# Attention normalised on the probabilities instead of the output, values turned into the stationary operand, in a one-core tokenizer, attention and expert kernel

## The chip, the cores and the metric

The kernel runs on one core of a Trainium2 chip. The metric is the device time of one execution in microseconds (us). The engines are PE (TensorE, matrix multiply), DVE (VectorE), ACT (ScalarE), POOL (GpSimd) and SP (SyncE, which only issues transfers). Each engine works through its own queue in order, and the kernel orders engines against each other with semaphores written by hand.

## The reference, cut to what matters

An input of 64 sequences is cut into 93 overlapping patches each (a strided product), goes through a causal attention layer with 8 heads of 64 and a bias by distance, and then through a two-of-sixteen expert layer. The change is inside the attention:

```python
tokens = jnp.einsum('bnpd,edp->bne', patches, Wr) + b           # 64 x 93 x 128
q = _split_heads(_proj(xp, wq1, wqd), b, n) * scale             # 8 heads of 64
k = _split_heads(_proj(xp, wk1, wkd), b, n)
v = _split_heads(_proj(xp, wv1, wvd), b, n)
sim = jnp.einsum('bhid,bhjd->bhij', q, k)                       # 93 x 93 per head
sim = sim + bias[None, None] * slopes[None, :, None, None]
attn = jax.nn.softmax(sim, axis=-1)
out = jnp.einsum('bhij,bhjd->bhid', attn, v)
return out.transpose(0, 2, 1, 3).reshape(b, n, INNER) @ wout.T
```

## The kernel before, in words

The 64 sequences form 16 groups of four. Phase 1 is a software pipeline over tiles: `step(t, u, f)` runs, for tile number t, six stages on six different groups: token product (group t, `tok`), layer norm (t-1, `norm`), the query, key and value projections with their three-tap convolution (t-2, `proj`), attention (t-3, `attn`), gating (t-4, `gate`), and the scatter of the rows to their experts (t-5, `scat`). Each tile has four steps s = 0 to 3, and each step takes one sequence through attention; n counts them (64 in all). Every engine has its own `step` with the same loops, and what stands in that text is its queue: nothing reorders it. t runs from 0 to 20; at t = 5 to 15 all six stages are on. At t = 17 and 18 attention still runs, without token product and norm. Phase 2 (experts, output) comes after, and waits until all rows are scattered.

In one step before the change:

- PE turns the shifted scores of the sequence before (L452, eight 93x93 transposes into `psS`), turns the values of this one (L469), multiplies turned probabilities by values with the probabilities stationary (L500, 65 columns: 64 values and a column of ones that yields the sum of the exponentials), forms the scores with bias (L516, L521), turns the normalised output (L544) and multiplies it by `wout` (L576). Between them stand three projection products `proj` and four token products `tok_taps`, each three matmuls at L406, L407 and L408.
- DVE takes the row maxima `rmax` of the scores (L876), subtracts them (L879, `shifted`), later takes the reciprocal of the sums (L867) and multiplies the output by it (L870, `attn`), runs two of three convolution taps for three blocks (`conv`, L831 and L834 each), and adds the result to the residual (L891). Once per tile come the layer norm statistics (`stats`, twice, L841 and L845), `route`, `choose`, `rank` and `place` (L898 to L954).
- ACT forms the exponentials while it moves the turned scores out of `psS` (L700, `probT`), moves the values (L710) and the turned output (L746), runs the third tap (`tap2`, L675) and rounds the input (`high`, L667, `x_hi`). `normalise` applies the two layer norms.
- POOL forms the rest of the rounded input (`low`, L1043, `x_lo`) and of the normalised tokens (L1096, `xnT_lo`), the small chain of a layer norm (L1066 to L1085, starting with `veps`) and issues the scatters (L1106), two per step, or eight in a row at the head of the tile where `norm` is off (t from 17).

`psP` has two buffers, so a projection product waits for the convolution two blocks back: `wait(pe, conv_done, (t - 2) * NBLK + (k - 1))`. The scatter waits for `slot_done`, which `place` gives, and PE turns `rw` (L536) after `rw_done`, the last result of `place`. That `rwT` is what phase 2 weighs the experts with.

Of the kernel before, what the change touches and what calls it, by code (L numbers as in the profile page):

```python
# [33 lines left out]
NT = 93  # L34
# [23 lines left out]
def build(nc, x, w_tok, b_tok, gamma, beta, wq, wk, wv, cq, ck, cv, w_out, w_gate, w1, w2,  # L58
# [3 lines left out]
    with ctx:  # L62
# [41 lines left out]
        vrow = [sb(f"vrow{u}", [NT, H, DH + 1]) for u in range(2)]  # L104
        rmax = sb("rmax", [NT, 2, 4])
        shifted = sb("shifted", [NT, 2, 4, NT])
        probT = sb("probT", [NT, 2, 4, NT])
        rden = sb("rden", [NT, 2, 4])
        attn = sb("attn", [NT, H * DH])
# [50 lines left out]
        with ExitStack() as phase1:  # L160
# [24 lines left out]
        psTot = psO[:, 0, 264:264 + E]  # L185
# [20 lines left out]
        consts_ready, zeros_ready, taps_ready, bias_cast, vones_ready, rwzero_ready = (  # L206
            sem("consts_ready"), sem("zeros_ready"), sem("taps_ready"), sem("bias_cast"),
            sem("vones_ready"), sem("rwzero_ready"))
# [11 lines left out]
        p_tr, p_evac, pv_mm, den_done, norm_done = (  # L220
            sem("p_tr"), sem("p_evac"), sem("pv_mm"), sem("den_done"), sem("norm_done"))
        a_tr, a_evac, out_mm, res_add = sem("a_tr"), sem("a_evac"), sem("out_mm"), sem("res_add")
# [180 lines left out]
        def _(pe):  # L403
# [38 lines left out]

            def step(t, u, f):
                for s in range(GB):
                    n = (t - 3) * GB + s
                    prev = f.attn and s > 0 or f.last and s == 0
                    if prev:

                        pe.wait_ge(shift_done, n)
                        for a in range(2):  # L450
                            for hh in range(4):
                                mm = nc.tensor.transpose(psS[:NT, a, hh * NT:(hh + 1) * NT], shifted[:, a, hh, :],  # L452
                                                         ident[:NT, :NT])
                            mm.then_inc(p_tr, 1)
                    if f.gate and s == 2:
                        wait(pe, hn_ready, t - 3)
                        wait(pe, norm_done, n - 1 if f.attn else B)
                        for b in range(GB):
                            mm = nc.tensor.transpose(psHn[:, b * NT:(b + 1) * NT], hn[u][:, b, :],
                                                     ident[:NT, :NT])  # L460
                        mm.then_inc(hnT_tr, 1)
                    if f.proj and s == 0:
                        proj(t, u, f, 3 * s)
                    if f.attn:
                        if s == 0:
                            pe.wait_ge(conv_done, (t - 2) * NBLK)
                        wait(pe, a_evac, n - 1)
                        for j in range(QB):
                            mm = nc.tensor.transpose(psV[:NT, j * 128:(j + 1) * 128],  # L469
                                                     qkv[1 - u][:, 2 * QB + j, s, :], ident[:, :])  # L470
                        mm.then_inc(v_tr, 1)
                    if f.proj and s > 0:
                        proj(t, u, f, 3 * s)
# [10 lines left out]
                    if f.tok:  # L484
                        tok_taps(t, s, 0, 1)
                    if prev:

                        pe.wait_ge(p_evac, n * 2)
                        pe.wait_ge(v_evac, n)
                        wait(pe, norm_done, n - 1)  # L490

                        wait(pe, res_add, n - 1)
                        if f.gate and s == 2:
                            wait(pe, hnT_evac, t - 3)
                        if f.gate and s == 3:
                            wait(pe, logit_copy, t - 3)
                        if f.scat and s == 0:
                            wait(pe, pos_done, t - 4)
                        for h in range(H):
                            mm = nc.tensor.matmul(psO[:NT, h // 4, (h % 4) * (DH + 1):(h % 4 + 1) * (DH + 1)],  # L500
                                                  probT[:, h % 2, h // 2, :], vrow[(s + 1) % 2][:, h, :],
                                                  start=True, stop=True)
                        mm.then_inc(pv_mm, 1)
# [6 lines left out]
                    if f.attn:  # L510

                        if s == 0 and isinstance(t, int) and t == 3:
                            pe.wait_ge(bias_cast, 4)
                        wait(pe, p_evac, n * 2)
                        for a in range(2):
                            nc.tensor.matmul(psS[:NT, a, 0:4 * NT], ident16[:NT, :NT], bias[:, a, :],  # L516
                                             start=True, stop=False, skip_group_check=True)
                        for hh in range(4):
                            for a in range(2):
# [8 lines left out]
                    if f.tok:  # L528
                        tok_taps(t, s, 1, 2)
                    if f.attn and prev:  # L530
                        pe.wait_ge(v_evac, n + 1)
                    if f.scat and s == 0:
# [5 lines left out]
                        if not prev:  # L538
                            mm.then_inc(rwT_tr, 1)
# [120 lines left out]
        def _(ac):  # L660
# [31 lines left out]
            def step(t, u, f):  # L692
                for s in range(GB):
# [19 lines left out]
                    if f.proj:  # L713
                        tap2(t, u, 3 * s)
# [458 lines left out]
```

## Time and profile before

| | |
|---|---|
| median of 3 runs | 843.96 us (843.8 to 844.66) |
| the profiled execution, its own time | 846.1 us |
| span of its instructions | 844.4 us |
| mean granted TensorE clock | 0.943 |
| PE busy | 752.6 us (89% of the span) |
| DVE busy | 615.9 us (73%) |
| ACT busy | 468.9 us (56%) |
| POOL busy | 383.3 us (45%) |
| one full tile of four steps | 36.61 us |

Busy times are of the whole span; phase 1 ends near 694 us and phase 2 follows. A PE that shows as busy is not necessarily at its peak, and the shares are means over stretches that have different limits, so the stretches are read one by one below. In the rows of groups, "busy" is the time of all instructions of the group, then the mean of one in ns.

### The profile page before, as it was taken

Reading aid. Unit: us, or ns where it says so; the run is one execution under the profiler, and the core shown is the slowest. Engines: PE = TensorE matmul, PEld = TensorE weight load, DVE = VectorE, ACT = ScalarE, POOL = GpSimd, SP = SyncE. Lnnn points to the kernel's source line nnn. Section 1 sums busy time; section 2 is a strip of 40 time slices with the busy share of each in tenths; the row PEclk is TensorE's granted clock in tenths of the full one; section 3 lists DMA queues with packets and bytes.
Section 4 is the critical chain, followed back from the end, with each engine's and each line's share of the span. In section 5 each row is a group of like instructions: output and inputs, shape, how many; then the busy total and the mean of one; then the engine's idle time right before and its main releaser. Section 6 shows DMA issues by size and latency. Waiting matters only on the chain. (4 is left out here: it accounts for less than half of the span.)

```text
span 844.4 us, 20971 instructions
## 1 busy us (share of the span) xinstructions
PE 752.6 (89%) x6670; PEld 696.4 (82%) x6670; DVE 615.9 (73%) x1621; ACT 468.9 (56%) x1021; POOL 383.3 (45%) x408
## 2 busy tenths in 40 slices
PE   5577999999999999999999999999786318999987
PEld 5466999999999999999999999977675208999983
DVE  2145778888888888888888888899573145888865
ACT  3345566656566665656666566555333107899950
POOL 3442243666556565555656556545241552222200
PEclk9787999999999999999999999999898658999989
DMA  6321123332112112111212211050000022222205
GB/s 190 99 72 46 47 72 117 102 104 64 48 47 66 47 47 65 50 46 46 68 46 50 65 48 48 19 208 20 10 15 6 19 69 73 64 62 62 62 17 145
DMA packets 42246, 53.89 MB, mean 64 GB/s; under 512 B 13651, under 2 KB 28947, under 8 KB 41680
## 3 DMA queue, kind: packets, MB, share of 16 engines
q1 hardware_dynamic: 26304, 37.13, 15.5%
q0 software_dynamic: 13120, 14.05, 6.0%
q10 hardware_dynamic: 2768, 2.00, 0.8%
q8 instruction: 32, 0.52, 0.3%
q14 instruction: 22, 0.18, 0.1%
HBM read 42.69 MB, written 10.26 MB: 63 GB/s over the span
## 5 line engine op out<-in xcount | busy, mean ns | idle before, releaser
L1106 POOL DMA_INDIRECT expert_rows<-hn,slot x128 | 167.7, 1310 | 92.5 <-DVE slot L951 59.9
L1043 POOL TENSOR_TENSOR x_lo<-x_raw,x_hi 128x752 fp32r<-128x752 f32 x64 | 114.9, 1795 | 151.7 <-ACT x_hi L667 151.7
L831 DVE SCALAR_TENSOR_TENSOR qkv<-ps,taps,qkv 128x368 f32<-128x368 f32 x192 | 114.0, 594 | 86.2 <-ACT qkv L675 84.6
L675 ACT ACTIVATE qkv<-ps,taps 128x372 f32<-128x372 f32 x192 | 108.6, 567 | 90.1 <-PE ps L408 89.8
L834 DVE SCALAR_TENSOR_TENSOR qkv<-ps,taps,qkv 128x364 f32<-128x364 f32 x192 | 114.6, 597 | 6.8
L406 PE MATMUL ps<-x_hi,wtok_hi 128*128 128x376 f32 x256 | 95.3, 372 | 11.3 <-DVE wtok_lo L811 9.0
L500 PEld LDWEIGHTS psO<-vrow,probT 93*93 93x93 f32 x1024 | 93.5, 162 | 4.7 <-ACT probT L700 3.2
L500 PE MATMUL psO<-vrow,probT 93*93 93x65 f32 x1024 | 93.9, 245 | 2.0 <-ACT probT L700 1.1
L407 PE MATMUL ps<-x_lo,wtok_hi 128*128 128x376 f32 x256 | 89.1, 348 | 0.0
L408 PE MATMUL ps<-x_hi,wtok_lo 128*128 128x376 f32 x256 | 89.0, 348 | 0.0
L576 PE MATMUL psO<-wout,attnT 128*93 128x128 f32 x512 | 70.6, 283 | 18.6 <-ACT attnT L746 15.8
L998 DVE TENSOR_REDUCE qkv<-qkv 128x512 f32 (+1 forms) x108 | 72.3, 681 | 19.1 <-ACT qkv L771 18.6
L406 PE MATMUL ps<-xnT_hi,wqkv_hi 128*128 128x372 f32 x192 | 78.0, 406 | 9.0 <-DVE qkv L834 5.0
L576 PEld LDWEIGHTS psO<-wout,attnT 128*93 128x93 f32 x512 | 63.8, 167 | 22.4 <-ACT attnT L746 19.8
L700 ACT ACTIVATE probT<-psS 93x372 f32<-93x372 f32 x128 | 54.4, 472 | 47.9 <-PE psS L452 47.6
L312 POOL DMA_DIRECT2D xs<-expert_rows x54 | 29.8, 552 | 82.2 <-PE psS L595 41.3
L407 PE MATMUL ps<-xnT_lo,wqkv_hi 128*128 128x372 f32 x192 | 65.0, 339 | 0.0
L408 PE MATMUL ps<-xnT_hi,wqkv_lo 128*128 128x372 f32 x192 | 65.0, 338 | 0.0
L876 DVE TENSOR_REDUCE rmax<-psS 93x8 f32<-93x744 f32 x64 | 59.2, 926 | 7.0 <-PE psS L521 5.9
L667 ACT ACTIVATE x_hi<-x_raw 128x752 fp32r<-128x752 f32 x64 | 52.7, 823 | 19.1 <-DMA x_raw<-in_x 14.4
L879 DVE TENSOR_TENSOR shifted<-psS,rmax 93x744 f32<-93x744 f32 x64 | 59.4, 929 | 5.2
L521 PEld LDWEIGHTS psS<-qkv 64*93 64x93 f32 x1024 | 47.2, 158 | 18.2 <-issue 18.2
(160 smaller groups left out, 1620.7 us busy)
## 6 DMA issues: line engine op xcount, KB each, us to landing
x_raw<-in_x SPq DMA_DIRECT2D x64, 376.0 KB, 3.2
w1s<-in_w POOLq DMA_DIRECT2D x8, 512.0 KB, 4.9
w<-in_w SPq DMA_DIRECT2D x4, 1024.0 KB, 10.3
xs<-expert_rows SPq DMA_DIRECT2D x54, 64.0 KB, 1.8
xs<-expert_rows POOLq DMA_DIRECT2D x54, 64.0 KB, 2.1
out<-resid SPq DMA_DIRECT2D x16, 160.0 KB, 2.4
expert_rows<-hn,slot POOLq DMA_INDIRECT x128, 3.5
qkv<-in_w_tok ACTq DMA_DIRECT2D x4, 256.0 KB, 6.7
```

The source lines that it names most:

```text
L406: nc.tensor.matmul(dst, w_hi, x_hi, start=start, stop=False)
L407: nc.tensor.matmul(dst, w_hi, x_lo, start=False, stop=False)
L408: return nc.tensor.matmul(dst, w_lo, x_hi, start=False, stop=stop)
L500: mm = nc.tensor.matmul(psO[:NT, h // 4, (h % 4) * (DH + 1):(h % 4 + 1) * (DH + 1)], probT[:, h % 2, h // 2, :], vrow[(s + 1) % 2][:, h, : ...
L576: mm = nc.tensor.matmul(psWout, attnT[:, j, :], wout[:, j, :], start=(j == 0), stop=(j == QB - 1))
L675: nc.scalar.activation(qkv[u][:, k, :, :], psP[(k + 1) % 2][:, 0:GT].rearrange("p (b n) -> p b n", n=NT), ACT.Copy, scale=taps[:, k, 2:3]) ...
L831: nc.vector.scalar_tensor_tensor(dst[:, :, 1:NT], src[:, :, 0:NT - 1], taps[:, k, 1:2], dst[:, :, 1:NT], ALU.mult, ALU.add).then_inc(tap1_ ...
L834: nc.vector.scalar_tensor_tensor(dst[:, :, 2:NT], src[:, :, 0:NT - 2], taps[:, k, 0:1], dst[:, :, 2:NT], ALU.mult, ALU.add).then_inc(conv_ ...
L879: nc.vector.tensor_tensor(shifted[:, :, :, :], heads(psS, NT), rmax[:, :, :].unsqueeze(3).broadcast_to([NT, 2, 4, NT]), ALU.subtract).then ...
L998: nc.vector.tensor_reduce(part[:, bass.ds(i, 1), :].rearrange("p i j -> p (i j)"), act[k][:, :].rearrange("p (j n) -> p j n", n=128), AXX, ...
L1043: nc.gpsimd.tensor_tensor(x_lo[u][:, 0:PIECE], x_raw[u][:, :], x_hi[u][:, 0:PIECE].bitcast(F32), ALU.subtract)\
L1106: nc.gpsimd.indirect_dma_start(rows, bass.IndirectOffsetOnAxis(slot[1 - u][:, c:c + 1], 0), hn[1 - u][:, c % GB, :], None)\
```

## The change

The exponentials are now formed before the turn, with queries on partitions, and divided by their row sums there. The pieces:

- ACT forms the exponentials in place in `prob` (93x744, two buffers), one instruction per step, and its move out of `psS` becomes a plain copy.
- DVE sums `prob` per head (`den`), takes the reciprocal and multiplies the four heads of the odd half (`a = 1`) in place; POOL multiplies the even half. The reciprocal and the product on the output, and the column of ones, are gone.
- PE turns the normalised probabilities and multiplies with the values stationary (64 columns wide, two halves of the array in turn), which gives the output already turned, in bank 0 of `psO`. The four transposes L544 are gone; ACT moves `psO` to `attnT`.
- The order of every queue in `step` is rewritten. DVE's `place` moves from the head of step 0 behind the product on the odd heads; ACT's `high` moves to the head, its `normalise` to the end of a step; on POOL the product on the even heads stands between `x_lo` and the scatters.

```diff
+            def turn_prob(f, s, n):
+                if f.attn:
+                    pe.wait_ge(shift_done, n + 1)
+                for a in range(2):
+                    pe.wait_ge((even_ready, odd_ready)[a], n)
+                    for hh in range(4):
+                        mm = nc.tensor.transpose(psS[:NT, a, hh * NT:(hh + 1) * NT], prob[(s + 1) % 2][:, a, hh, :],
+                                                 ident[:NT, :NT])
+                    mm.then_inc(p_tr, 1)
+            def weigh(s, n):
+                pe.wait_ge(p_evac, n * 2)
+                pe.wait_ge(v_evac, n)
+                wait(pe, a_evac, n - 1)
+                wait(pe, res_add, n - 1)
+                for hh in range(4):
+                    for a in range(2):
+                        mm = nc.tensor.matmul(psO[64 * a:64 * a + 64, 0, hh * NT:(hh + 1) * NT],
+                                              vrow[(s + 1) % 2][:, 2 * hh + a, :], probT[:, a, hh, :],
+                                              start=True, stop=True)
+                mm.then_inc(pv_mm, 1)
...
                     if f.scat and s == 0:
                         wait(pe, rw_done, t - 4)
-                        wait(pe, a_evac, n - 1 if prev else B)
...
                     if prev:
-                        pe.wait_ge(norm_done, n)
-                        for j in range(QB):
-                            mm = nc.tensor.transpose(psV[:, j * NT:(j + 1) * NT], attn[:, j * 128:(j + 1) * 128],
-                                                     ident[:NT, :NT])
-                        mm.then_inc(a_tr, 1)
+                        weigh(s, n)
...
+                    if f.attn:
+                        ac.wait_ge(shift_done, n + 1)
+                        p = prob[s % 2][:, :, :, :].rearrange("p a h n -> p (a h n)")
+                        nc.scalar.activation(p, p, ACT.Exp).then_inc(exp_done, 1)
...
-                        nc.vector.tensor_tensor(attn[:, :].rearrange("p (a h d) -> p a h d", a=2, d=DH),
-                                                o[:, :, :, 0:DH],
-                                                rden[:, :, :].unsqueeze(3).broadcast_to([NT, 2, 4, DH]),
-                                                ALU.mult).then_inc(norm_done, 1)
...
+                    if f.attn:
+                        dve.wait_ge(exp_done, n + 1)
+                        wait(dve, even_ready, n)
+                        nc.vector.tensor_reduce(den[:, :, :], prob[s % 2][:, :, :, :], AXX, ALU.add).then_inc(sum_done, 1)
+                        dve.wait_ge(sum_done, n + 1)
+                        nc.vector.reciprocal(rden[:, :, :], den[:, :, :]).then_inc(rden_done, 1)
+                        dve.wait_ge(rden_done, n + 1)
+                        p = prob[s % 2][:, 1, :, :]
+                        nc.vector.tensor_tensor(p, p, rden[:, 1, :].unsqueeze(2).broadcast_to([NT, 4, NT]), ALU.mult)\
+                            .then_inc(odd_ready, 1)
+                    if f.scat and s == 0:
+                        place(t - 5, 1 - u)
...
+                    if f.attn:
+                        pool.wait_ge(rden_done, n + 1)
+                        p = prob[s % 2][:, 0, :, :]
+                        nc.gpsimd.tensor_tensor(p, p, rden[:, 0, :].unsqueeze(2).broadcast_to([NT, 4, NT]), ALU.mult)\
+                            .then_inc(even_ready, 1)
                     if f.scat and f.norm:
                         scatter(t - 5, u, 2 * s, 2)
```

DVE's queue in step 0 of a full tile (t = 5), before, from the end of the tile before; `wden` to `rw` is `place`, the two rows with `qkv` are one `conv`:

```order
L891 TENSOR_TENSOR resid<-psO,resid 93x128
L934 TENSOR_SCALAR wden<-egap 93x4
L936 RECIPROCAL wts<-wden 93x4
...
L954 TENSOR_TENSOR rw<-wsel 93x4x16
L831 SCALAR_TENSOR_TENSOR qkv<-ps,taps,qkv 128x4x92
L834 SCALAR_TENSOR_TENSOR qkv<-ps,taps,qkv 128x4x91
L867 RECIPROCAL rden<-psO 93x8
L870 TENSOR_TENSOR attn<-psO,rden 93x512
L876 TENSOR_REDUCE rmax<-psS 93x8
L879 TENSOR_TENSOR shifted<-psS,rmax 93x744
```

And the same engine in the same step of the changed kernel:

```order
L848 TENSOR_REDUCE rmax<-psS 93x8
L851 TENSOR_TENSOR prob<-psS,rmax 93x744
L825 SCALAR_TENSOR_TENSOR qkv<-ps,taps,qkv 128x4x92
L828 SCALAR_TENSOR_TENSOR qkv<-ps,taps,qkv 128x4x91
L867 TENSOR_REDUCE den<-prob 93x8
L869 RECIPROCAL rden<-den 93x8
L872 TENSOR_TENSOR prob<-prob,rden 93x372
L928 TENSOR_SCALAR wden<-egap 93x4
...
L945 CAST slot<-slotf 93x8
L948 TENSOR_TENSOR rw<-wsel 93x4x16
L825 SCALAR_TENSOR_TENSOR qkv<-ps,taps,qkv 128x4x92
```

The maxima moved to the head of the step, one `conv` now stands between the subtraction and the new sum, and `place` moved from the head of the step to behind seven other instructions (a `...` in the first fence leaves out `place`'s middle rows).

PE's queue of the changed kernel in the same step, from the turn of the probabilities; L543 is the turn of `rw`, L493 is `weigh`, and three rows with `ps` are one product:

```order
L481 MATMUL psS<-ident,prob 93x93 x8
L406 MATMUL ps<-xnT_hi,wqkv_hi 128x372
L407 MATMUL ps<-xnT_lo,wqkv_hi 128x372
L408 MATMUL ps<-xnT_hi,wqkv_lo 128x372
L406 MATMUL ps<-x_hi,wtok_hi 128x376
L407 MATMUL ps<-x_lo,wtok_hi 128x376
L408 MATMUL ps<-x_hi,wtok_lo 128x376
L543 MATMUL psV<-ident,rw 128x93
L493 MATMUL psO<-probT,vrow 64x93 x8
```

The turn of `rw` stands in front of `weigh`, and so in front of everything that PE does in the rest of that step; before, it stood behind the product of probabilities and values.

POOL's queue of the changed kernel at the head of tile 17 and up to tile 18, where `norm` is off (L1096 is here the product on the even heads):

```order
L1106 DMA expert_rows<-hn,slot 97408x128 x10
L1096 TENSOR_TENSOR prob<-prob,rden 93x372
L1072 TENSOR_SCALAR veps<-mv 93x4
L1074 TENSOR_SCALAR nmean<-mv 93x4
L1077 TENSOR_TENSOR rstd<-veps,half 93x4
L1080 TENSOR_TENSOR shift<-nmean,rstd 93x4
L1096 TENSOR_TENSOR prob<-prob,rden 93x372 x3
```

Eight of the ten scatters in the first row belong to tile 17; the product of step 0 has moved in behind them, where before only the layer norm chain stood.

## Rows read from the trace of the kernel before

**Rows 1.** Windows: us, then busy time of each engine, clock, DMA
```profile
293.60:330.21 36.61, 36.61 (x347) 34.59 (x346) 30.99 (x88) 22.37 (x47) 21.70 (x22) 1.00 0.20 53
553.36:585.77 32.41, 29.82 (x297) 25.62 (x295) 30.29 (x88) 18.01 (x41) 14.61 (x18) 1.00 0.26 91
585.77:625.34 39.57, 31.97 (x284) 28.36 (x284) 28.20 (x78) 15.56 (x34) 12.22 (x13) 0.87 0.05 11
625.34:652.59 27.25, 18.94 (x188) 16.70 (x189) 12.27 (x41) 7.79 (x18) 9.55 (x11) 0.87 0.06 15
```

**Rows 2.** Timeline, weight loads of PE in one step: start, us
```profile
339.79 1.49 PEld L500 LDWEIGHTS psO<-vrow,probT 93*93 93x93 f32 x16
341.20 0.18 PEld L516 LDWEIGHTS psS<-bias,ident 93*93 93x93 bf16 x2
341.66 0.74 PEld L521 LDWEIGHTS psS<-qkv 64*93 64x93 f32 x16 [0.28 <-issue]
342.49 0.19 PEld L406 LDWEIGHTS ps<-xnT_hi,wqkv_hi 128*128 128x128 f32 x1
...
343.99 0.47 PEld L544 LDWEIGHTS psV<-ident,attn 93*128 93x128 f32 x4
...
345.37 0.98 PEld L576 LDWEIGHTS psO<-wout,attnT 128*93 128x93 f32 x8
346.30 0.77 PEld L452 LDWEIGHTS psS<-ident,shifted 93*93 93x93 f32 x8
```

**Rows 3.** Timeline, DVE in steps 2, 3, 0 and 1
```profile
320.60 0.21 DVE L898 COPY logit<-psO 93x64 f32<-93x64 f32 x1
...
322.88 0.59 DVE L831 SCALAR_TENSOR_TENSOR qkv<-ps,taps,qkv 128x368 f32<-128x368 f32 x1
...
324.02 0.19 DVE L867 RECIPROCAL rden<-psO 93x8 f32<-93x8 f32 x1
...
324.86 0.92 DVE L876 TENSOR_REDUCE rmax<-psS 93x8 f32<-93x744 f32 x1
325.90 0.93 DVE L879 TENSOR_TENSOR shifted<-psS,rmax 93x744 f32<-93x744 f32 x1
326.75 0.21 DVE L925 TENSOR_TENSOR pos<-psO,base 93x64 f32<-93x64 f32 x1
...
329.60 0.28 DVE L891 TENSOR_TENSOR resid<-psO,resid 93x128 f32 x1
329.80 0.21 DVE L934 TENSOR_SCALAR wden<-egap 93x4 f32<-93x4 f32 x1
...
331.03 0.22 DVE L954 TENSOR_TENSOR rw<-wsel 93x64 f32<-93x64 f32 x1
...
339.32 0.87 DVE L841 BATCH_NORM_STATS2 stat<-resid 93x6 f32 x4
...
340.64 0.57 DVE L831 SCALAR_TENSOR_TENSOR qkv<-ps,taps,qkv 128x368 f32<-128x368 f32 x1
```

**Rows 4.** Instructions of one line: min/median/max ns, first and last start
```profile
L811 DVE TENSOR_TENSOR wtok_lo<-qkv,wtok_hi x4: 678/686/1918, 7.0 to 10.3; 128x512 fp32r<-128x512 f32 x4
```

**Rows 5.** Groups of the profile page, ACT
```profile
L675 ACT ACTIVATE qkv<-ps,taps 128x372 f32<-128x372 f32 x192 | 108.6, 567 | 90.1 <-PE ps L408 89.8
L667 ACT ACTIVATE x_hi<-x_raw 128x752 fp32r<-128x752 f32 x64 | 52.7, 823 | 19.1 <-DMA x_raw<-in_x 14.4
```

**Rows 6.** Timeline, POOL
```profile
6.60 1.76 POOL L1043 TENSOR_TENSOR x_lo<-x_raw,x_hi 128x752 fp32r<-128x752 f32 x1 [5.59 <-ACT x_hi L667]
...
327.04 1.00 POOL L1096 TENSOR_TENSOR xnT_lo<-xnT,xnT_hi 128x372 fp32r<-128x372 f32 x1
...
340.92 0.19 POOL L1077 TENSOR_SCALAR veps<-mv 93x4 f32<-93x4 f32 x1 [3.20 <-DVE mv L845]
...
342.61 1.81 POOL L1043 TENSOR_TENSOR x_lo<-x_raw,x_hi 128x752 fp32r<-128x752 f32 x1
...
583.42 1.29 POOL L1106 DMA_INDIRECT expert_rows<-hn,slot  x1 [2.40 <-DVE slot L951]
```

More of the change, by code:

```diff
@@ new lines, in values @@
+            def values(t, u, f, s, n):
+                if s == 0:
+                    pe.wait_ge(conv_done, (t - 2) * NBLK)
+                wait(pe, v_evac, n)
+                if f.scat and s == 1:
+                    wait(pe, rwT_evac, t - 4)
+                for j in range(QB):
+                    mm = nc.tensor.transpose(psV[:NT, j * 128:(j + 1) * 128],
+                                             qkv[1 - u][:, 2 * QB + j, s, :], ident[:, :])
+                mm.then_inc(v_tr, 1)
+            def turn_prob(f, s, n):
+                if f.attn:
+                    pe.wait_ge(shift_done, n + 1)
+                for a in range(2):
+                    pe.wait_ge((even_ready, odd_ready)[a], n)
[3 more added lines that the diff above has]
+                    mm.then_inc(p_tr, 1)
@@ L446, in step @@
                     prev = f.attn and s > 0 or f.last and s == 0
[L447 to L452, printed above, removed]
-                                                         ident[:NT, :NT])
[L454 to L462, printed above, removed]
+                    if f.attn:
+                        scores(t, u, s, n)
+                    if f.proj:
                         proj(t, u, f, 3 * s)
                     if f.attn:
-                        if s == 0:
-                            pe.wait_ge(conv_done, (t - 2) * NBLK)
-                        wait(pe, a_evac, n - 1)
-                        for j in range(QB):
[L469 to L473, printed above, removed]
+                        values(t, u, f, s, n)
                     if f.norm and s == 0:
@@ L483, in step @@
                         mm.then_inc(tok_tr, 1)
[L484 to L503, printed above, removed]
                     if f.norm and s == 3:
@@ L572, in step @@
                         pe.wait_ge(a_evac, n)
-                        if f.gate and s == 3:
-                            wait(pe, base_done, t - 3)
                         for j in range(QB):
@@ L752, in step @@
                         tap2(t, u, 3 * s + 2)
+                    if f.norm and s == 2:
+                        normalise(t - 1, rstd, shift, xn, ln_shift, xn_ready)
+                    if f.gate and s == 1:
+                        wait(ac, scattered[u], (t - u - 4) * (16 * GB))
+                        normalise(t - 4, rstd2, shift2, hn[u], ln2_shift, hn_ready)
                     if isinstance(t, int) and t == 0 and s == GB - 1:
@@ L1059, in step @@
                 for s in range(GB):
+                    n = (t - 3) * GB + s
                     if f.scat and not f.norm and s == 0:
```

160 lines of the change are left out of this document (74 added, 86 removed).

## The prediction, made before the changed kernel was run

> **What bounds it now.** I read the windows first, cut at the same point of two successive tiles. In a full tile (36.61 us) PE is busy for all of it and DVE for 30.99 us; with the token product over, a tile takes 32.41 us with DVE busy 30.29 and PE 29.82 [rows 1]. So the eleven full tiles (t = 5 to 15) and the two before them are bound by PE, with DVE close behind, and tile 16 by DVE. Next the timelines, for what one block costs in its queue, counted from its start to the start of the next. PE: the score block 1.29 us (341.20 to 342.49), three products 1.50 (0.50 each), probabilities times values 1.41, `wout` 0.93, the four transposes of the output at most 0.47, the eight of the scores some 0.7 [rows 2]. DVE: maxima 1.04, subtraction 0.85, one `conv` 1.14, reciprocal with product on the output 0.84, residual 0.20; and once per tile `place` 1.45, `stats` twice 1.32, `route` with `choose` 2.28, `rank` 0.21 [rows 3]. Check: 4 x (1.04 + 0.85 + 3 x 1.14 + 0.84 + 0.20) + 6.58 = 32.0 us, which is the 32.41 us of the tile that DVE bounds.
>
> **The change, part by part.**
>
> PE loses 0.45 us per step with the transposes. `weigh` has no row of its kind. The nearest are the scores: eight pairs in two halves of the array take 0.83 us, with 0.28 us of idle time ahead of them as the array changes its form, so 1.1; if the halves don't overlap it stays at the old 1.41. I take 1.1. PE alone would give 36.6 - 4 x 0.75 = 33.6 us per tile.
>
> DVE loses 0.84 and gets: the sum over 744 elements, priced as the maxima over as many, 1.04; the reciprocal, 0.19 and a small gap, 0.23; the product on the odd heads. The last from two rows: 512 elements took 0.686 us [rows 4], 744 took 0.93, so 1.05 ns per element and 0.54 for 372, of which the next instruction covers 0.08 as it does behind the subtraction: 0.46. A step is then 7.24 instead of 6.35 us, and a tile 4 x 7.24 + 6.58 = 35.5 us. DVE, not PE, bounds the tile from here, and its best case is 1.1 us under today's 36.6.
>
> ACT gets 0.82 us per step (its 752-column copy took 0.823 [rows 5]), 22.37 + 3.3 of some 40 us: not a bound, but the sum on DVE waits for it.
>
> POOL gets the even heads, 1.00 us per step by the 372-column `x_lo` kind [rows 6], 21.70 + 4 of 40 us: hidden in itself.
>
> **Waits that are new.** I lay out each step from the start of the maxima (0). The subtraction ends at 1.9. PE turns the previous probabilities (2.6), does two products (3.6), `weigh` (4.7), two products (5.7), `wout` (6.6) and the next scores (7.9; with the tail of a matmul 8.1). Where DVE has more than that to do, DVE sets the step.
>
> Step 0: PE's turn of `rw` stands ahead of `weigh` and waits for the end of `place`, which now stands behind the odd heads. ACT has `tap2` (0.57), the values and the residual copy (512 columns each, some 0.6 between the rows of 372 and 752 columns [rows 5]) ahead of the exponentials. The first product of the step is through at 0.7, so these end at 2.5 and the exponentials at 3.3; sum 4.35, reciprocal 4.6, odd heads 5.05, `place` 6.5. PE then needs `rw` 0.15, `weigh` 1.1, two products 1.0, `wout` 0.93, scores 1.3: 11.1 us in all. Queued behind that wait are the product whose `conv` DVE wants next, and the scores. Before, `place` ran at the head of step 0, straight behind the residual (329.60, 329.80 [rows 3]).
>
> Step 1: 7.24 + 1.32 = 8.6 us. Step 2: 8.6 + 1.6 (`route`) = 10.2. Step 3: DVE 7.24 + 0.67 + 0.21 = 8.1, PE 8.1 and the ranking's matmuls 0.3: 8.4. Together 38.3 us, 1.7 more than now.
>
> Then the collisions. One of four equal DVE subtractions with both inputs in SBUF took 1918 ns where the others took 686 [rows 4]. It started at 7.0, while POOL was in `x_lo` from 6.60 to 8.36 [rows 6]: it ended 0.56 us after POOL, as if it had begun there. The product on the odd heads is such an instruction. In steps 1 and 2 POOL starts its layer norm chain 0.3 us after DVE has gone on from `stats` (340.92 [rows 6], 340.64 [rows 3]), and `x_lo` follows 1.7 us later for 1.8 us (342.61 [rows 6]). From the maxima: DVE goes on at 1.9 + 1.32 = 3.2, the chain starts at 3.5, `x_lo` runs from 5.2 to 7.0; the odd heads would start at 3.2 + 1.14 + 1.04 + 0.23 = 5.6 and end at 7.4 instead of 6.2. That is 1.2 us in each of the two steps, and DVE is the bound in both. In step 0 POOL's even heads (5.1 to 6.1) hold up `place`, 0.6; in step 3 `x_lo` and `xnT_lo` hold up `choose`, 0.3. In all 3.3 us: 38.3 + 3.3 = 41.6.
>
> The Trainium skill states the same in SBUF — State Buffer, section "SBUF: two separate sides": the pair of ports that VectorE and GpSimd share is taken for a whole instruction, and a VectorE instruction needs it with two SBUF inputs. The trace agrees, 1918 against 686 ns. By that rule the sum, with one SBUF input, is free of it; and if the even heads took the pair first when `x_lo` ends, the odd ones would lose a further 1.0 us.
>
> **The sum.** Full tiles: 11 x (41.6 - 36.6) = 55. Tile 4 (no scatter, so no wait for `rw`): step 0 8.3, then 9.8, 11.4, 8.7, 38.2: +2. Tile 3 +1. Tile 16, without token product: 10.7 + 8.6 + 10.2 + 8.4 against 32.4: +5. Tiles 17 and 18: eight scatters now stand ahead of the even heads of step 0, and wait for `slot`, from 6.3. Eight take 8 x 1.6 = 12.7 us (a scatter 1.29 [rows 6] and 0.3 to the next), then the heads 1.0: ready at 20. PE needs 6.3 from there through turn, copy, `weigh`, `wout` and scores. So steps 0 and 1 take 26 us; with steps 2 and 3 (8.9 and 8.2) tile 17 is 43.4 against 39.57, tile 18 with 26 and 8.5 is 34.5 to its third step against 27.25 [rows 1]. That is +11, and `place` for tile 19 starts 3 later: +14, of which I take 12 since these tiles have other slack. Phase 2 unchanged. 55 + 2 + 1 + 5 + 12 = 75. The profiled execution took 846.1 us (span 844.4), 2 above the median of the runs: 921 there, 919 as a median.
>
> **Rivals.**
> - *The collisions hardly bite* (`x_lo` lies elsewhere, or the delay is shared): tiles of 38.3, 11 x 1.7 = 19, tiles 3 and 4 nothing, 5 and 12 as before: +36, 880. For it: `x_lo` is placed by several waits, and only one clear case is in the trace. Against: the window of 1.8 us is wide. Chance 0.24, with all that lies between 865 and 895.
> - *TensorE's clock falls too.* In tile 17, with PE busy 31.97 of 39.57 us, the mean granted clock was 0.87; tile 16, at 29.82 of 32.41, kept 1.00 [rows 1]. The changed tile would have PE busy near 34 of 41.6. A quarter of the tiles' PE path at a lower clock adds 1 to 3 us each: 935 to 955. Chance 0.11.
> - *Faster.* DVE packs without a wait: 35.5 us per tile, 13 x 1.1 = -14 us, with the last tiles at +5: 835. It decides where the new waits of a tile stay under 1.1 us together; the wait for `rw` alone costs 2. For it: PE really has less to do, and ACT and POOL have room. Chance 0.06, up to 842.
> - *Nothing to measure* (within 0.2%, which is what a measurement of this kernel can tell from no change): the same with 1 us of waits per tile; 0.03.
>
> **Numbers.** The layout with collisions has 0.56, its own range 895 to 940. With the rival without collisions inside, 868 to 945 leaves about 2 in 10 out. Slower 0.91, same 0.03, faster 0.06.
>
> **What would show it.** Windows of a full tile near 41.6 us, DVE busy over 85% and PE under 90%. PE idle ahead of the turn of `rw`, released by DVE's `rw`, 3 us per full tile. The odd product with a median near 0.55 us and a maximum near 1.8, long in steps 1 and 2. `den` near 0.93 us, eight pairs of `weigh` near 0.83. PE idle ahead of the turn of `prob` in tiles 17 and 18, released by POOL, some 8 us each. Wrong would make it: `weigh` at twice its price matters little; an `x_lo` that comes before the odd product costs 2.4 us of my tile; an exponential that waits behind other work on ACT would add to every step.

## The result, and the profile after

The changed kernel takes 970.5 us (median of 4 runs, 963.67 to 977.35) against 843.88 us of the kernel before: 1.150 times as long, 95% interval 1.141 to 1.160. The sign was forecast; the size was not: 970.5 lies above the range of 868 to 945 and 51 us above the 919 expected. The four runs lie 13.7 us apart, and the interval of their ratio is 8 us wide to either side, so a difference from 970.5 below is sure to some 8 us only; where a trace shows the same saving, its number stands beside it. The profiled execution took 966.65 us, its span is 964.9 us.

The head of its page: busy time, share of the span, instructions; then the granted clock in 40 slices.

```profile
span 964.9 us, 20730 instructions
...
PE 771.0 (80%) x6414; PEld 676.5 (70%) x6414; DVE 715.3 (74%) x1683; ACT 518.3 (54%) x1085; POOL 453.4 (47%) x472
...
PEclk9899989898979998999998899899787555999999
```

No engine is busy as large a share of the time as PE was before (89%): the kernel now waits. The windows, cut at PE's turn of `rw` in successive tiles, answer to [rows 1] (us, busy time and instructions of PE, PEld, DVE, ACT, POOL, clock, DMA share, GB/s):

```profile
285.32:330.95 45.63, 37.98 (x329) 33.34 (x329) 38.29 (x92) 25.51 (x51) 26.15 (x25) 0.92 0.16 43
330.95:377.41 46.46, 36.86 (x329) 32.03 (x329) 38.34 (x92) 25.43 (x51) 26.15 (x25) 0.93 0.16 42
```

A full tile takes 46 us where it took 36.61 and was forecast at 41.6. DVE is busy for 38.3 of them; forecast were 35.5 plus the time in collisions. The clock, 1.00 before, is 0.92. Where the time went along the program is read from an instruction that closes each tile in both kernels, the last addition to the residual. Timeline of the changed kernel at the ends of tiles 4, 15, 16 and 18, then of the kernel before:

```profile
139.36 0.28 DVE L885 TENSOR_TENSOR resid<-psO,resid 93x128 f32<-93x128 f32 x1
...
642.28 0.28 DVE L885 TENSOR_TENSOR resid<-psO,resid 93x128 f32<-93x128 f32 x1
...
682.51 0.28 DVE L885 TENSOR_TENSOR resid<-psO,resid 93x128 f32<-93x128 f32 x1
...
776.84 0.29 DVE L885 TENSOR_TENSOR resid<-psO,resid 93x128 f32<-93x128 f32 x1 [1.77 <-PE psO L574]
```

```profile
146.47 0.28 DVE L891 TENSOR_TENSOR resid<-psO,resid 93x128 f32<-93x128 f32 x1
...
549.37 0.28 DVE L891 TENSOR_TENSOR resid<-psO,resid 93x128 f32<-93x128 f32 x1
...
581.78 0.28 DVE L891 TENSOR_TENSOR resid<-psO,resid 93x128 f32<-93x128 f32 x1
...
655.96 0.29 DVE L891 TENSOR_TENSOR resid<-psO,resid 93x128 f32<-93x128 f32 x1 [1.27 <-PE psO L576]
```

Between the first two of each lie the eleven full tiles: 502.9 us after (45.7 each), 402.9 before (36.6 each), so +100.0. The next tile took 40.2 against 32.4 us, +7.8; the two behind it 94.3 against 74.2, +20.2. At the end of tile 4 the changed kernel is 7.1 us ahead. Together +120.9 us, and by that the second part of the kernel starts later (818.50 against 697.69); its own length has not changed.

One full tile on DVE, cut to the rows that matter. Step 1 starts at 291.30, step 2 at 301.06, step 3 at 314.03, the next tile's step 0 at 323.91 and its step 1 at 335.42:

```profile
291.30 0.93 DVE L848 TENSOR_REDUCE rmax<-psS 93x8 f32<-93x744 f32 x1
...
295.62 0.92 DVE L867 TENSOR_REDUCE den<-prob 93x8 f32<-93x744 f32 x1
...
296.80 1.86 DVE L872 TENSOR_TENSOR prob<-prob,rden 93x372 f32<-93x372 f32 x1
...
301.06 0.92 DVE L848 TENSOR_REDUCE rmax<-psS 93x8 f32<-93x744 f32 x1
...
312.33 1.77 DVE L901 TENSOR_TENSOR gap<-top 93x4 f32<-93x4 f32 x1
314.03 0.92 DVE L848 TENSOR_REDUCE rmax<-psS 93x8 f32<-93x744 f32 x1
...
323.91 0.93 DVE L848 TENSOR_REDUCE rmax<-psS 93x8 f32<-93x744 f32 x1
...
328.51 0.54 DVE L872 TENSOR_TENSOR prob<-prob,rden 93x372 f32<-93x372 f32 x1
328.97 0.77 DVE L928 TENSOR_SCALAR wden<-egap 93x4 f32<-93x4 f32 x1
```

And POOL in the same tile:

```profile
296.48 1.78 POOL L1037 TENSOR_TENSOR x_lo<-x_raw,x_hi 128x752 fp32r<-128x752 f32 x1
298.23 1.10 POOL L1096 TENSOR_TENSOR prob<-prob,rden 93x372 f32<-93x372 f32 x1
...
312.28 1.79 POOL L1037 TENSOR_TENSOR x_lo<-x_raw,x_hi 128x752 fp32r<-128x752 f32 x1
...
328.56 1.16 POOL L1096 TENSOR_TENSOR prob<-prob,rden 93x372 f32<-93x372 f32 x1 [3.06 <-DVE rden L869]
```

Three DVE instructions last about as long as POOL needs to the end of its own: the odd product (1.86 us, alone 0.54), as forecast; `wden` (0.77, alone 0.15), as forecast for `place` though a different line of it; and `gap`, 93 x 4 elements, 1.77 us instead of 0.14, in a place for which the prediction had no collision. It began 0.05 us behind an `x_lo`.

PE in the same stretch, behind the wait for `rw` and behind the turn in step 3:

```profile
285.32 0.41 PE L543 MATMUL psV<-ident,rw 93*128 93x93 f32 x1 [2.53 <-DVE rw L948]
...
287.59 0.52 PE L407 MATMUL ps<-x_lo,wtok_hi 128*128 128x376 f32 x1
287.90 0.52 PE L408 MATMUL ps<-x_hi,wtok_lo 128*128 128x376 f32 x1
288.21 0.51 PE L406 MATMUL ps<-xnT_hi,wqkv_hi 128*128 128x372 f32 x1
...
316.06 1.41 PE L481 MATMUL psS<-ident,prob 93*93 93x93 f32 x8 [3.45 <-DVE prob L851]
...
317.64 0.51 PE L407 MATMUL ps<-xnT_lo,wqkv_hi 128*128 128x372 f32 x1
317.95 0.51 PE L408 MATMUL ps<-xnT_hi,wqkv_lo 128*128 128x372 f32 x1
318.25 0.52 PE L406 MATMUL ps<-x_hi,wtok_hi 128*128 128x376 f32 x1
```

In both stretches the products follow one another at 0.31 us; elsewhere in this trace it is 0.17 (273.29, 273.46, 273.63). That is the lower of the clock's two levels, 1.2 instead of 2.4 GHz. Not every wait is followed by it: behind the same wait in the next tile, 2.68 us at 330.95, the products stand 0.17 apart. And in the tile shown the lower level had begun before the wait, at 282.28, behind a wait of 2.00 us for `prob` at 280.61. The waits of PE in all, by what ended them (us, times, longest):

```profile
PE psS L481 <- DVE prob L851: 69.2, 39, 4.0
PE psV L543 <- DVE rw L948: 38.8, 16, 3.2
...
PE psS L481 <- POOL prob L1096: 12.0, 2, 6.2
```

### The profile page after: what moved, and what is told of

Same layout as the page of the kernel before. It is cut to its first block and busy times, and to the rows that moved or that the text cites. A ratio compares the mean times of both kernels' runs of the same rounds, so it can differ in the third digit from the quotient of the medians.

```text
span 964.9 us, 20730 instructions
## 1 busy us (share of the span) xinstructions
PE 771.0 (80%) x6414; PEld 676.5 (70%) x6414; DVE 715.3 (74%) x1683; ACT 518.3 (54%) x1085; POOL 453.4 (47%) x472
## 5 line engine op out<-in xcount | busy, mean ns | idle before, releaser
L1096 POOL TENSOR_TENSOR prob<-prob,rden 93x372 f32<-93x372 f32 x64 | 70.3, 1099 | 140.5 <-DVE rden L869 140.4
L481 PE MATMUL psS<-ident,prob 93*93 93x93 f32 x512 | 63.6, 274 | 81.2 <-DVE prob L851 69.2
L481 PEld LDWEIGHTS psS<-ident,prob 93*93 93x93 f32 x512 | 53.5, 179 | 96.6 <-DVE prob L851 83.4
L406 PE MATMUL ps<-x_hi,wtok_hi 128*128 128x376 f32 x256 | 101.5, 396 | 11.0 <-DVE wtok_lo L805 8.8
L719 ACT ACTIVATE prob<-prob 93x744 f32<-93x744 f32 x64 | 52.7, 823 | 66.9 <-DVE prob L851 66.4
L574 PE MATMUL psO<-wout,attnT 128*93 128x128 f32 x512 | 80.0, 308 | 1.8 <-ACT attnT L737 1.7
L574 PEld LDWEIGHTS psO<-wout,attnT 128*93 128x93 f32 x512 | 75.1, 189 | 3.8 <-ACT attnT L737 2.8
L493 PE MATMUL psO<-probT,vrow 93*64 93x93 f32 x1024 | 69.9, 291 | 1.3 <-ACT probT L724 1.1
L493 PEld LDWEIGHTS psO<-probT,vrow 93*64 93x64 f32 x1024 | 56.4, 168 | 17.8 <-issue 12.8
L872 DVE TENSOR_TENSOR prob<-prob,rden 93x372 f32<-93x372 f32 x64 | 67.0, 1046 | 2.2
```

The source lines that it names most:

```text
L406: nc.tensor.matmul(dst, w_hi, x_hi, start=start, stop=False)
L493: mm = nc.tensor.matmul(psO[64 * a:64 * a + 64, 0, hh * NT:(hh + 1) * NT], vrow[(s + 1) % 2][:, 2 * hh + a, :], probT[:, a, hh, :], start= ...
L574: mm = nc.tensor.matmul(psWout, attnT[:, j, :], wout[:, j, :], start=(j == 0), stop=(j == QB - 1))
```

## The experiments

Four kernels first, to price what the prediction had named: the collision of the odd product, the wait for `rw`, the scatters. All times are medians; ratios are to the kernel before, beside which each ran (844.0 to 844.5 us).

**x_lo first.** On POOL, `low` stands ahead of the layer norm chain instead of behind it.

```
                     if f.scat and not f.norm and s == 0:
                         scatter(t - 5, u, 0, 2 * GB)
+                    if f.tok and f.more(t, s):
+                        low(t * GB + (s + 1), (s + 1) % 2)
...
-                    if f.tok and f.more(t, s):
-                        low(t * GB + (s + 1), (s + 1) % 2)
```

> Only the order of POOL's queue changes: in every step x_lo is formed ahead of the layer norm chain, so that in steps 1 and 2 it is over before DVE's product on the odd heads begins. Theory of the collisions: the 26 long odd products (1.75 to 1.89 us) become 0.54, worth 26 x 1.25 = 33 us, of which DVE as the bound of those steps gives back nearly all: 25 to 33 us faster than the changed kernel (970.5), the full tiles near 43 us. Rival, that the long products only cover other waits: the odd products are short but the time moves by less than 8 us. The collision of the gap instruction in step 2 (1.76 us) and that of wden in step 0 (0.77) stay under both.

Measured: 936.06 us, ratio 1.107 (1.103 to 1.111), 34.4 us less. The line of the odd product, min/median/max, in the changed kernel and here:

```profile
L872 DVE TENSOR_TENSOR prob<-prob,rden x64: 541/542/1887, 71.5 to 772.6; 93x372 f32<-93x372 f32 x64
```

```profile
L872 DVE TENSOR_TENSOR prob<-prob,rden x64: 541/542/544, 71.9 to 745.6; 93x372 f32<-93x372 f32 x64
```

No long one is left. In the changed kernel the 64 of them were busy for 67.0 us, 32.3 more than 64 x 0.542: nearly all that the time fell by. `gap` still collides (median 1266 ns).

**rw late.** PE's turn of `rw`, and ACT's copy of it, move to the end of step 0, behind the scores.

```
-                    if f.scat and s == 0:
-                        wait(pe, rw_done, t - 4)
...
                         mm.then_inc(out_mm, 1)
+                    if f.scat and s == 0:
+                        wait(pe, rw_done, t - 4)
...
```

> PE's turn of rw moves behind the wout product at the end of step 0, and ACT's move of rwT behind its last tap2. Theory of the rw wait: PE no longer idles 3.0 us per full tile ahead of weigh in step 0, and step 0 (now 12.7 us, against 11.7 laid out) falls to about 9.3; 11 to 14 tiles x 3.0 to 3.4 = 33 to 45 us faster than 970.5. As the idle time goes, TensorE should stay at full clock in that stretch. Rival, that DVE bounds step 0 anyway, with the wait only in its shadow: under 12 us.

Measured: 936.48 us, ratio 1.110 (1.107 to 1.113), 34.0 us less, 2.1 in each of 16 tiles. The prediction had said that this wait costs 2 us a tile. The 2.1 are what is left of more: by the traces, step 0 of the eleven full tiles takes 35.9 us less in all, and step 3 takes 14.8 us more, where PE now waits some 3.5 us for `prob` and then runs at the lower level (217.96 to 227).

**Scatters behind.** In the two last tiles POOL takes the even heads before the eight scatters.

```
-                    if f.scat and not f.norm and s == 0:
-                        scatter(t - 5, u, 0, 2 * GB)
...
                             .then_inc(even_ready, 1)
+                    if f.scat and not f.norm and s == 0:
+                        scatter(t - 5, u, 0, 2 * GB)
```

> In tiles 17 and 18 the eight scatters of step 0 go behind the product on the even heads instead of ahead of it. Theory: PE no longer waits for POOL's even heads there (12.0 us in two waits), 10 to 14 us faster than 970.5. Rival, that the scatters end later and hold back the layer norm chain of step 1 by as much: under 3 us.

Measured: 959.61 us, ratio 1.136 (1.132 to 1.140), 10.9 us less; the prediction had 12. The traces show it where it was expected: from the maxima of step 0, tile 17 takes 40.9 instead of 46.7 us, and tile 18 34.3 instead of 38.7 to its last step. POOL and PE in the changed kernel, the last of eight scatters, the even heads, and PE behind them:

```profile
700.39 1.28 POOL L1106 DMA_INDIRECT expert_rows<-hn,slot  x1 [0.30 <-issue]
701.70 0.82 POOL L1096 TENSOR_TENSOR prob<-prob,rden 93x372 f32<-93x372 f32 x1
```

```profile
702.66 1.53 PE L481 MATMUL psS<-ident,prob 93*93 93x93 f32 x8 [5.81 <-POOL prob L1096]
```

**All three.**

> The three moves together. If the three causes are apart they add: 68 to 90 us off 970.5, 880 to 902. If PE's wait for rw and the collisions cover each other, less: 915 or more. What DVE has to do itself (35.5 us per tile by the sum of its blocks, plus the collisions of gap and wden) leaves it slower than before the change, 844.

Measured: 879.23 us, ratio 1.041 (1.038 to 1.044), 91.3 us less, where the three singly give 79.3. Each came out near its price in the prediction, 2.4 x 13 + 2 x 16 + 12 = 75 us, which is as much as its whole sum. Yet 35 us remain. So there are costs that it did not name. Two candidates were in the trace: `gap`, and the clock.

**gap late, alone.** `gap` moves from the end of `route` in step 2 to behind the mask in `choose`, in step 3; nothing else.

```
-                nc.vector.tensor_tensor(gap[:, :], top[:, :, 1], top[:, :, 0], ALU.subtract).then_inc(gap_done, 1)
...
                                         hot[:, GB:, :], ALU.add).then_inc(mask_done, 1)
+                nc.vector.tensor_tensor(gap[:, :], top[:, :, 1], top[:, :, 0], ALU.subtract).then_inc(gap_done, 1)
```

> The changed kernel as it is, with gap alone moved from the end of route to behind the mask in choose. It prices the one collision that the prediction's list did not have: gap at 1760 ns where it was 141. Theory (the wait is on the path of step 2, whose probabilities TensorE waits for): 1.6 us less in 16 tiles, 26 us, and the clock a little up: 935 to 950. Rival (gap's wait is hidden, or the following max waits instead for something else): within 6 us of 970.5.

Measured: 939.05 us, ratio 1.113 (1.110 to 1.116), 31.5 us less. In its trace:

```profile
L913 DVE TENSOR_TENSOR gap<-top x16: 152/155/1003, 130.4 to 771.9; 93x4 f32<-93x4 f32 x16
```

Step 2 now takes 11.27 us (334.81 to 346.08) instead of 12.96. Over the eleven full tiles step 2 takes 18.8 us less and step 3, where PE had waited behind `gap`, 6.8 less. Moving one instruction of 93 x 4 elements is worth as much as the collision of all odd products. On the kernel with all three mends, the same move:

> The three mends together, and the operation gap moved from the end of route to behind the mask in choose, in step 3, away from GpSimd's x_lo. Theory (the 1.27 us that gap took in place of 0.14 is on the path): 1.1 us less in about 17 tiles: 8 to 19 us less than 879.2, so 860 to 871. Rival (the wait is only moved to whatever VectorE's next operation with two inputs is, or step 3 has no room): within 4 us of 879.2.

Measured: 857.71 us, ratio 1.017 (1.014 to 1.021), 21.5 us less. The expectation's upper end was 19.

**PE kept busy.** The changed kernel, with matmuls that depend on nothing ahead of the two waits.

```
+            def idle_work(count):
+                for _ in range(count):
+                    nc.tensor.matmul(psTok[:, 384:512], ident16[:, :], ident16[:, :], start=True, stop=True,
+                                     skip_group_check=True)
...
+                        idle_work(16)
                         turn_prob(f, s, n)
...
+                        idle_work(40)
                         wait(pe, rw_done, t - 4)
```

> The changed kernel with idle matmuls on TensorE (ident16 against itself into a stretch of psTok that nothing reads): 16 ahead of every turn of the probabilities and 40 ahead of the wait for rw. They depend on nothing, so they run while TensorE waits for VectorE (3.78 us ahead of a turn in step 3, 3.02 us ahead of the turn of rw); the results are unused. Theory (the idle stretches halve TensorE's clock for the products behind them): granted clock back to 0.98 or more in a full tile, the odd and even heads' weight loads back to 0.17 us from about 0.31, some 1.0 to 1.2 us less in each of steps 0 and 3, so 20 to 35 us less than the 970.5 us: 936 to 950. Rival 1 (VectorE's collisions set the length, the low clock is in their shadow): clock up, time within 6 us of 970.5. Rival 2: the idle matmuls, where VectorE is in time, stand in TensorE's way: 16 of them take some 0.9 us in 68 steps, the time rises by 20 us or more.

They write into the bank in which the token product sums, and change the numbers that come out of it, against what the expectation says of that stretch. The instructions of the rest are the same. Measured: 951.8 us (942.0 to 956.1), ratio 1.129 (1.124 to 1.133), 18.7 us less, just under the 20 expected, with 1664 matmuls more. PE in step 3 of a tile:

```profile
312.67 0.90 PE L486 MATMUL psS<-ident,prob 93*93 93x93 f32 x8 [2.55 <-DVE prob L857]
...
313.60 0.33 PE L407 MATMUL ps<-xnT_lo,wqkv_hi 128*128 128x372 f32 x1
313.77 0.33 PE L408 MATMUL ps<-xnT_hi,wqkv_lo 128*128 128x372 f32 x1
```

The turn takes 0.90 instead of 1.41 us, products stand 0.17 apart, and step 3 takes 8.45 us (310.64 to 319.09) instead of 9.88. `gap` is as long as it was (median 1765 ns), so this gain is the clock's, less what the idle matmuls themselves cost. Over the eleven full tiles steps 3 take 6.6 us less and steps 0 6.3; the tiles from 16 gain as well (17: 44.1 instead of 46.7 us). The trace is that of the fastest of the four runs.

On the mended kernel the same device does harm:

> The three mends, gap late, and 16 idle matmuls ahead of each turn of the probabilities. Theory (in the mended kernel too the halved clock behind the wait for VectorE's subtraction costs the step): granted clock near 1.00, 10 to 25 us less than the same kernel without the idle matmuls: 840 to 860. Rival 1 (VectorE sets the step): clock up, time within 4 us. Rival 2 (the idle matmuls delay the turn): 10 us or more longer.

Measured: 870.58 us, ratio 1.030 (1.027 to 1.033), 12.9 us more than without. The clock rises from 0.92 to 0.941, but the waits there are shorter and the idle matmuls stand ahead of work that was ready: rival 2.

**Without the row sum.** What DVE's new sum costs, on the kernel with three mends and on that with `gap` late too. `den` is one column plus 1.0, so the true sums are left out.

```
-   nc.vector.tensor_reduce(den[:, :, :], prob[s % 2][:, :, :, :], AXX, ALU.add).then_inc(sum_done, 1)
+   nc.vector.tensor_scalar(den[:, :, :], prob[s % 2][:, :, :, 0], 1.0, None, ALU.add).then_inc(sum_done, 1)
```

> The three mends together (x_lo first, rw turned late, scatters behind the even product) with the sum over the 93 columns left out: VectorE writes one column of the probabilities plus 1.0 to den, an operation on 93 x 8 in place of the reduction of 93 x 744 at 0.914 us, so the probabilities are divided by a wrong number and the rest is done as before. Theory (VectorE's own work is what lengthens a step once the collisions are gone): about 0.75 us less in each of 68 steps, some 45 to 50 us less than 879.2: 829 to 840, at or under the kernel before. Rival (the wait for GpSimd's half or TensorE sets the step): less than 20 us of that shows, 860 or more.

Measured: 862.63 us, ratio 1.022 (1.019 to 1.024), 16.6 us less instead of 45 to 50. The theory fell: of the 48 us that DVE was spared (58.5 to 10.7 busy) a third showed.

> The three mends and gap late (857.7 us), with the sum over the 93 columns left out as in the run on the three mends alone (one column plus 1.0 in its place, so the probabilities are divided by a wrong number). Theory (with gap out of the way VectorE is still what a step waits for, 33 us of work in a tile of 36 to 37): 25 us or more less, 833 or under. Rival (TensorE, with its rounded products through ScalarE's tap, is now as long as VectorE; in the run without the sum VectorE waited 64.0 us in all for ScalarE's tap where it had waited 33.9 here): less than 15 us, 843 or more.

Measured: 834.73 us, ratio 0.989 (0.986 to 0.992), 23.0 us less: nearer to the theory's 25 than to the rival's 15, within neither. DVE's wait for ACT's tap says where the rest went; the kernel with `gap` late, and the same without the sum:

```profile
L825 DVE SCALAR_TENSOR_TENSOR qkv<-ps,taps,qkv 128x368 f32<-128x368 f32 x192 | 113.0, 588 | 33.9 <-ACT qkv L673 33.9
```

```profile
L825 DVE SCALAR_TENSOR_TENSOR qkv<-ps,taps,qkv 128x368 f32<-128x368 f32 x192 | 113.3, 590 | 59.8 <-ACT qkv L673 59.4
```

DVE is spared 48 us and waits 26 more for a tap that hangs on PE's products: the two engines are nearly level, and taking work off one shows by half. This version alone is faster than the kernel before, by 1.1%, and only because it leaves the sum out.

**All on DVE.** The even heads' product moves from POOL to DVE.

```
-                        p = prob[s % 2][:, 1, :, :]
...
+                        for a, ready in enumerate((even_ready, odd_ready)):
+                            p = prob[s % 2][:, a, :, :]
+                            nc.vector.tensor_tensor(p, p, rden[:, a, :].unsqueeze(2).broadcast_to([NT, 4, NT]),
+                                                    ALU.mult).then_inc(ready, 1)
...
-                        nc.gpsimd.tensor_tensor(p, p, rden[:, 0, :].unsqueeze(2).broadcast_to([NT, 4, NT]), ALU.mult)\
-                            .then_inc(even_ready, 1)
```

> The three mends and gap late, with the even heads' product on VectorE too (two operations of 0.54 us one after the other; GpSimd has no product left). It costs VectorE 0.54 us in each of 64 steps and takes away GpSimd's 0.80 us, its waits and what it shares SBUF with. Theory (VectorE is near the bound of a step, GpSimd's product is hidden behind its convolutions): 64 x 0.3 to 0.54 = 20 to 35 us more, 878 to 892. Rival (the hand-over to GpSimd and back cost as much as they save): within 6 us of 857.7.

Measured: 854.09 us, ratio 1.012 (1.008 to 1.017), 3.6 us less than with POOL's help. The rival's number came true, but not its reason: DVE does 29.2 us more products (63.9 against 34.7) and the kernel is no slower, and by the traces that is because a stall went away with the change. Idle time marked "issue" ahead of `rmax` was 12.4 us and is none; 10.6 of it had stood in three places, where the loop goes back to its start (heads of tiles 8, 10 and 12). Away from the loop's edges (tiles 5, 6, 13, 14, 15) a tile takes 37.1 us here and 36.3 with POOL's help; from 7 to 12 it takes 37.3 against 38.9. So POOL's help is worth 0.7 us in a full tile, and the stall took it back. `wden`, with POOL's product and without it:

```profile
L928 DVE TENSOR_SCALAR wden<-egap x16: 156/770/770, 139.4 to 691.0; 93x4 f32<-93x4 f32 x16
```

```profile
L929 DVE TENSOR_SCALAR wden<-egap x16: 155/159/161, 142.9 to 688.6; 93x4 f32<-93x4 f32 x16
```

This shows what held `wden`, by taking it away: 0.61 us in most of the 16 tiles, some 8 us of DVE's time.

> The version with all of the normalisation on VectorE (854.1 us), its two products of 93 x 372 (538 ns each) made one of 93 x 744 (about 0.93 us, as the subtraction of that size), so 0.15 us less for VectorE in each of 64 steps; the even heads are ready 0.39 us later than they were, the odd ones 0.15 us earlier. Theory (VectorE's work, 35 of 37.3 us in a tile, is the bound): 64 x 0.15 = 10 us less, 842 to 847, level with the kernel before. Rival (TensorE waits for the subtraction and has its products to do; the even heads' delay takes it back): within 3 us of 854.1.

Measured: 865.35 us, ratio 1.025 (1.022 to 1.028), 11.3 us more, against both theories. DVE's product is as short as expected (929 ns for two of 538), and a tile away from the loop's edges takes 37.0 us instead of 37.1. The idle time ahead of `rmax` is back, 7.3 us "issue" and 8.4 for the scores where there were none and 5.9; these 9.8 us are near to the difference. With the stall in both, one product on DVE (865.4) is 7.6 us behind the split between DVE and POOL (857.7).

## Why the prediction was wrong

Its terms against what the trace shows, tiles cut at the residual: full tiles 55, measured 100.0; the tiles before them +3, measured -7.1; tile 16 5, measured 7.8; the last two 12, measured 20.2. Two errors, of 10 us in the start and of 8 in the last tiles, nearly cancel; what is left of the error is the length of a full tile. By its steps, from the maxima of one to those of the next, summed over the eleven full tiles (us):

| | forecast | measured | with PE kept busy |
|---|---|---|---|
| step 0 | 11 x 11.7 = 128.7 | 136.8 | 130.5 |
| step 1 | 11 x 9.8 = 107.8 | 106.6 | 106.7 |
| step 2 | 11 x 11.4 = 125.4 | 141.3 | 141.5 |
| step 3 | 11 x 8.7 = 95.7 | 117.6 | 111.0 |

- **What bounds it, what moves.** Right. PE waits 2.3 to 2.8 us for `rw` in each full tile, `den` 915 ns, the odd product 541, sixteen `weigh` loads with their idle time 1.05 us. POOL's product alone took 0.80, not 1.00.
- **The waits.** Right in place, and near in size by their own runs: 2.1 us a tile for `rw` (2 forecast), though as the net of a larger gain in step 0 and a loss in step 3; 10.9 us for the scatters (12 forecast).
- **The ends of phase 1.** "Tile 4 ... +2" was 3.5 (40.1 against 36.6). But at the start of tile 4 the changed kernel was 10.6 us ahead (99.28 against 109.92), for which the prediction had +1; what gained it in the filling of the pipeline no run looked into. The last two tiles, laid out at 43.4 and 34.5 us, took 46.7 and 38.7, with the granted clock at 0.69 where it was 0.87 in the kernel before; with PE kept busy they took 44.1 and 35.5. Here too the layout was right and the clock missing.
- **"In steps 1 and 2 ... 1.2 us in each of the two steps".** Right: 1.3 us each time, two to a tile. The rule of the Trainium skill, SBUF — State Buffer, section "SBUF: two separate sides", agrees with the rows. The further 1.0 us it allowed for did not come: the odd product ran ahead of POOL's even one.
- **"In all 3.3 us: 38.3 + 3.3 = 41.6". The step that failed.** In the tile shown the steps took 11.5, 9.8, 13.0 and 9.9 us, against 11.7, 9.8, 11.4 and 8.7 forecast. Step 2 is 1.6 us longer there: the list of collisions looked at the large DVE instructions and at `choose`, and passed over `gap`, a DVE subtraction with two SBUF inputs behind which `rmax` is queued. The prediction had `route` end at the end of step 2, and left out that POOL, with its scatters done, starts the next `x_lo` just there. Price alone: 31.5 us, of which 18.8 are seen in step 2 of the full tiles.
- **Step 3, "DVE 7.24 + 0.67 + 0.21 = 8.1, PE 8.1": right durations at the wrong clock.** PE had idled 3.45 us for `rmax` and the subtraction, held up by `gap`, and the turn and the products behind it ran at the lower level: 9.9 us, and 8.45 with PE kept busy. The low clock in all places together, step 0 and the last tiles with it, has a price alone of 18.7 us. The prediction had the clock as a rival, at 0.11, and as a change to some tiles; it took all durations of its own layout from rows at full clock, though that layout itself has PE idle in every tile. A rival's mechanism that the main case sets off belongs in the main case.
- **The loop's edge.** Not thought of. The loop holds tiles 6 to 13, two to a turn, and goes back to its start three times. In the changed kernel's trace tiles 8, 10 and 12 begin so, with 2.5 to 2.6 us:

```profile
278.56 0.93 DVE L848 TENSOR_REDUCE rmax<-psS 93x8 f32<-93x744 f32 x1 [2.53 <-issue]
```

The 7.6 us lie in the steps 3 ahead of them, and the steps 0 behind them take 12.7 to 12.8 instead of 11.5 us, 3.8 in all. Of the 44.7 us by which the eleven tiles exceed their forecast, 15.9 are in step 2 (`gap`), 21.9 in step 3 (7.6 of them the loop's edge), 8.1 in step 0, and -1.2 in step 1. Keeping PE busy took 6.6 us out of step 3 and 6.3 out of step 0; the rest of the excess in step 3, some 8 us, is not priced by any run. This is an account, not a test: the prices singly overlap, as `gap` late (31.5 us) also takes part of PE's idle time away, and what the loop's edge costs no run priced alone.
- **Rival "collisions hardly bite", rival "faster".** Both refuted: the collisions were worth about 34 us by the odd product and 31.5 by `gap`.

What makes the mended kernel, with `gap` late, 1.7% slower than the kernel before lies at the loop's edge, and the cause of that stays open. Its full tiles take from 36.1 to 40.1 us. Two of them:

```profile
290.82:330.91 40.09, 34.89 (x333) 30.59 (x329) 34.19 (x92) 25.22 (x51) 26.58 (x26) 1.00 0.20 55
330.91:367.82 36.91, 34.92 (x333) 30.55 (x329) 34.14 (x92) 25.18 (x51) 26.59 (x26) 1.00 0.19 46
```

The short one is as long as a tile before (36.61); the long one holds the edge of the loop, where `rmax` waits 3.52 us (at 326.21) while PE, its products done, idles too. Eleven tiles of 1.1 us more on average (37.7 against 36.6) are 12 of the 13.9 us, and the three waits of 3.5 us are most of these. So a tile of the new form, freed of its collisions, is level with one of before where the stall is absent, and no shorter.

## What to carry to other kernels

When work is put on GpSimd or taken between engines, list every VectorE instruction that can fall beside each GpSimd instruction, the smallest too: what is lost is the rest of GpSimd's instruction, not a share of one's own. Then lay the order out again with the TensorE waits that it makes, and price the TensorE work behind each long wait at the low clock. And before two versions are compared by their times alone, compare their tiles: split between two engines and not split, the short product here gave 857.7 and 854.1 us, while tile by tile the split was 0.7 us ahead wherever the stall at the loop's edge was absent.

## What the runs showed of the hardware

- **`wden` waits though one of its inputs is a constant.** A VectorE operation of 93 x 4 with a scalar took 768 to 770 ns beside GpSimd's product and 159 without it. The sum `den` with one input was never lengthened (915 ns). The section of the Trainium skill named above covers the first with its clause on operations that use both ports of VectorE; the prediction had read only the clause on two inputs. The cast `idxf` in `choose` did the same in the kernel with `gap` late, beside `xnT_lo`: 0.59 us at 434.36, 0.16 in the changed kernel.
- **A stall at the loop's edge.** Idle time marked "issue" ahead of `rmax`: none before, 7.6 us in the changed kernel, 10.6 with the three mends and `gap` late, none with all products on VectorE as two, 7.3 with them as one; where it occurs, it stands at each of the three returns of the loop, and at none in the other two. Runtime: NRT & Kernel Launch, section "Instruction fetch mechanics" of the Trainium skill, says that a taken branch can make the sequencer wait for instructions. That fits the place; no run here varied the code's size or layout alone, so the cause is not shown. Between the last two versions it makes 7.3 of 11.3 us, as much as some of the changes under test.
- **The clock answers waits that are shorter than a step, but not each of them.** Idle time of 3.45 us was followed by some 3 us at the lower level (316.06 to past 318.88). A wait of 2.00 us and one of 2.53 close behind it had the lower level from 282.28 to 288.8, and 2.68 us at 330.95, with products at the higher level ahead of it, had none.
